# A gated-feed-forward kernel: casts and quantisation of its down stage shared out anew, and products that nobody reads put ahead of it

## What is computed

```python
x = x + jnp.tanh(g_xattn[0]) * _L0_xattn_ref(_layernorm(x, axis=-1), ctx_1024, ctx_1024, L0_xattn_w, L0_xattn_u)
x = x + jnp.tanh(g_ffn[0]) * _L0_ffn_ref(_layernorm(x, axis=-1), L0_ffn_clip_x, L0_ffn_clip_down, ...)

def _act_fake_quant(x, clip_factor):
    scale = jax.nn.sigmoid(clip_factor) * jnp.max(jnp.abs(x)) / QMAX
    return jnp.clip(_ste_round(x / scale), -QMAX - 1.0, QMAX) * scale
...
xq = _act_fake_quant(x, clip_x[0])
gate = jnp.einsum('bsh,ih->bsi', xq, _weight_fake_quant(w_gate))
up = jnp.einsum('bsh,ih->bsi', xq, _weight_fake_quant(w_up))
h = _act_fake_quant(jax.nn.silu(gate) * up, clip_down[0])
return jnp.einsum('bsi,hi->bsh', h, _weight_fake_quant(w_down))
```

## Time and profile before

| | |
|---|---|
| median of 3 runs | 224.18 us (224.08 to 225.59) |
| profiled execution | 224.41 us |
| its span, first to last instruction | 222.9 us |
| mean granted TensorE clock | 0.911 |
| busy: PE, DVE, ACT, POOL | 160.8, 171.0, 156.0, 138.5 us |

### The profile page before, as it was taken

How to read it: one execution, slowest core, us unless ns; L and a number is a source line. 1 busy time by engine, 2 the same in 40 slices (tenths; PEclk the granted TensorE clock), 3 DMA queues, 4 the chain that set the end, 5 groups by cost and what they waited for, 6 DMA issues and landing times.

```text
span 222.9 us, 3218 instructions
## 1 busy us (share of the span) xinstructions
PE 160.8 (72%) x1034; PEld 113.4 (51%) x1034; DVE 171.0 (77%) x344; ACT 156.0 (70%) x234; POOL 138.5 (62%) x157
## 2 busy tenths in 40 slices
PE   0002997799999999974066567949999952989960
PEld 0001342799999999964055452404343411766630
DVE  0689357445856779998679669677999998999992
ACT  3496596446698796996479966855988962899400
POOL 3467300425979999893688807992686670019991
PEclk9999999999999999999655766988999997699995
DMA  3999989999999878300000000000000000003458
GB/s 105 321 370 349 307 263 294 305 285 301 285 285 268 227 204 222 96 1 1 0 0 0 0 3 1 0 0 3 0 0 0 0 1 3 0 0 128 157 195 276
DMA packets 43327, 29.29 MB, mean 131 GB/s; under 512 B 2224, under 2 KB 43056, under 8 KB 43312
## 3 DMA queue, kind: packets, MB, share of 16 engines
q1 hardware_dynamic: 43168, 28.84, 44.8%
q10 hardware_dynamic: 144, 0.26, 0.3%
HBM read 24.65 MB, written 4.46 MB: 131 GB/s over the span
## 4 chain that ended last, share of the span: by engine, by line
PE 35%; DVE 17%; ACT 17%; POOL 11%; issue 9%; SPq 4%; DMA 4%; DVEq 1%; POOLq 0%; ACTq 0%
PE ps L955 11%; PE ps L988 8%; PE ps L884 6%; PE ps L868 5%; DMA hidden<-in_ctx 4%; SPq L261 4%; PE ps L908 3%; POOL x_all L389 3%; DVE h_space L831 2%; POOL hidden L382 2%; ACT hidden L563 2%; ACT silu_out L608 2%; DVE hidden L792 2%; DVE silu_out L700 2%; ACT h_space L608 2%
## 5 line engine op out<-in xcount | busy, mean ns | idle before, releaser
L884 PE MATMUL ps<-hidden 128*128 128x128 f32 (+1 forms) x512 | 58.5, 275 | 4.0 <-DVE hidden L638 2.5
L884 PEld LDWEIGHTS ps<-hidden 128*128 128x128 f32 x512 | 57.7, 192 | 5.2 <-issue 3.3
L868 PE MATMUL ps<-hidden,flip 128*128 128x512 f32 x32 | 16.7, 683 | 21.2 <-DMA hidden<-in_ctx 21.0
L389 POOL TENSOR_TENSOR x_all<-x_all,silu_out 128x512 f32<-128x512 f32 x16 | 24.4, 1536 | 10.8 <-DVE silu_out L700 10.7
L803 DVE TENSOR_REDUCE h_peaks<-hidden (+2 forms) x24 | 26.0, 1123 | 4.0 <-POOL hidden L433 3.2
L988 PE MATMUL ps<-wdT,z_t 128*128 128x256 bf16 (+1 forms) x192 | 25.3, 288 | 2.6 <-ACT z_t L622 2.6
L691 DVE SCALAR_TENSOR_TENSOR h_space<-z_t,ps 128x256 f32<-128x256 f32 x32 | 19.2, 599 | 10.3 <-PE ps L884 10.2
L908 PE MATMUL ps<-ident,hidden 128*128 128x128 f32 x64 | 14.3, 401 | 14.8 <-POOL hidden L413 11.1
L622 ACT ACTIVATE z_t<-h_space 128x1024 bf16<-128x1024 int8 (+3 forms) x12 | 20.1, 1756 | 6.6 <-DVE h_space L831 6.6
L988 PEld LDWEIGHTS ps<-wdT,z_t 128*128 128x128 bf16 (+1 forms) x192 | 17.2, 102 | 10.7 <-issue 4.8
L608 ACT ACTIVATE silu_out<-ps,mix_scale 128x1024 f32<-128x1024 f32 (+1 forms) x18 | 18.4, 1020 | 5.6 <-PE ps L955 2.6
(11 more groups left out here) (99 smaller groups left out, 331.6 us busy)
## 6 DMA issues: line engine op xcount, KB each, us to landing
hidden<-lag_w SPq DMA_DIRECT2D x26, 512.0 KB, 5.7
x_all<-in_x SPq DMA_DIRECT2D x8, 512.0 KB, 9.0
hidden<-in_ctx SPq DMA_DIRECT2D x8, 512.0 KB, 8.8
out<-x_all SPq DMA_DIRECT2D x16, 256.0 KB, 2.1
xq<-in_L_ffn_w_down SPq DMA_DIRECT2D x1, 704.0 KB, 5.7
xq<-in_L_ffn_w_gate SPq DMA_DIRECT2D x1, 640.0 KB, 6.5
h_space<-in_L_ffn_w_up SPq DMA_DIRECT2D x1, 640.0 KB, 5.7
lag_w<-up_out ACTq DMA_DIRECT2D x1, 255.0 KB, 7.8
```

Source lines behind the costliest of these rows:

```text
L389: nc.gpsimd.tensor_tensor(xs, xs, mixed[:, m % 2, :, :].rearrange("p c b -> p b c"), ALU.add).then_inc(s["x1_done"], 1)
L868: last = nc.tensor.matmul(turned(g)[:, half], flip[:, :], ring[g % SLOTS][:, half], start=True, stop=True)
L884: last = nc.tensor.matmul(ps[:, j % BANKS, c * 2 * SEQS:end * 2 * SEQS], lag_tile(j)[:, c, :], ekp[:, (j * CK + c) * 2 * SEQS:(j * CK + en ...
```

## The change

Five things change in the down stage, and block 0 keeps its six pieces.

1. Vector quantises only tiles 0 to 3 of blocks 1 to 3, in two pieces of 2048 columns.
2. ScalarE quantises tile 4 and the half tile (1536 columns, the new line 638) and then casts these, then tiles 0 and 1, then tile 2.
3. Pool casts tile 3 of blocks 1 to 3 (the new line 444): block 1's ahead of all additions, block 2's ahead of addition 4, block 3's ahead of addition 8.
4. TensorE multiplies a block in three parts, tiles 4 and 5, tiles 0 and 1, tiles 2 and 3; the last waits for ScalarE and for Pool. A semaphore, `row_read`, keeps block 1 from bank 6 until `down_row` has been read.
5. TensorE runs 14 products of 512 columns in bank 5 before the transpose of the peak and 8 after `row_ps`, which nobody reads (`idle_products`).

```diff
--- before.py
+++ after.py
@@ -159,13 +159,17 @@
         def z_bank(g):
             return (2, 6, 0)[g % 3]
 
-        def pieces(b):
-            return [(k, k + 1) for k in range(KA)] if b == 0 else [(0, KA // 2), (KA // 2, KA)]
-
-        def piece(b, k):
-
-            before = 0 if b == 0 else KA + 2 * (b - 1)
-            return before + (k + 1 if b == 0 else 1 + k // (KA // 2))
+
+
+        ACT_Q = 4
+
+        def quantised(b):
+
+            return KA + 2 * b
+
+        def act_cast(b):
+
+            return KA + 3 * b
 
         EVEN = (KA + 1) // 2
         ODD = KA // 2
@@ -222,9 +226,9 @@
             "top_done", "topT",
 
             "scale_x", "x8_done", "xq_done", "xq_cast", "gate_done", "up_done", "silu_done", "up_kept", "h_even", "h_odd",
-            "hpeak_done", "h_top_done", "h_topT", "row_ps",
-
-            "h8_done", "hq_done", "down_done", "ffn_done", "sum_done", "dve_sum_done", "out_done")}
+            "hpeak_done", "h_top_done", "h_topT", "row_ps", "row_read",
+
+            "h8_done", "h8_act", "hq_done", "hq_pool", "down_done", "ffn_done", "sum_done", "dve_sum_done", "out_done")}
 
         x_in = [sem(f"x_in{g}") for g in range(GROUPS)]
         ring_in = [sem(f"ring_in{i}") for i in range(SLOTS)]
@@ -434,7 +438,15 @@
                                             up_even[i % 2], ALU.mult).then_inc(s["h_even"], 1)
 
 
+            def cast_h(b):
+                pool.wait_ge(s["h8_done"], quantised(b))
+                wait(pool, s["down_done"], 4 * (b - 1))
+                nc.gpsimd.tensor_copy(hq[:, b % 2, 3 * BT:4 * BT], h8[:, b % 2, 3 * BT:4 * BT]).then_inc(s["hq_pool"], 1)
+
+            cast_h(1)
             for n in pool_sums:
+                if n in (4, 8):
+                    cast_h(n // 4 + 1)
                 pool.wait_ge(s["ffn_done"], n + 1)
                 xs = x_all[:, n * 2 * C:(n + 1) * 2 * C]
                 nc.gpsimd.tensor_tensor(xs, xs, ffn[n // 4 % 2][:, n % 4, :], ALU.add).then_inc(s["sum_done"], 1)
@@ -613,13 +625,25 @@
                                              scale=mix_scale[:, 1, k:k + 1]).then_inc(s["up_kept"], 1)
 
 
-            for b in range(BLOCKS):
-                for k, end in pieces(b):
-                    act.wait_ge(s["h8_done"], piece(b, k))
-                    if k == 0:
-                        wait(act, s["down_done"], 4 * (b - 1))
-                    cols = slice(k * BT, min(end * BT, HB))
-                    nc.scalar.activation(hq[:, b % 2, cols], h8[:, b % 2, cols], ACT.Copy).then_inc(s["hq_done"], 1)
+            def cast_h(b, k, end):
+                cols = slice(k * BT, min(end * BT, HB))
+                nc.scalar.activation(hq[:, b % 2, cols], h8[:, b % 2, cols], ACT.Copy).then_inc(s["hq_done"], 1)
+
+            for k in range(KA):
+                act.wait_ge(s["h8_done"], k + 1)
+                cast_h(0, k, k + 1)
+            for b in range(1, BLOCKS):
+                first, last = ACT_Q * BT, HB
+                wait(act, s["hq_done"], KA if b == 2 else act_cast(b - 2) if b > 2 else 0)
+                nc.scalar.activation(h8[:, b % 2, first:last], hidden[:, b * HB + first:b * HB + last], ACT.Copy,
+                                     scale=S["inv_h"]).then_inc(s["h8_act"], 1)
+                act.wait_ge(s["h8_act"], b)
+                wait(act, s["down_done"], 4 * (b - 1))
+                cast_h(b, ACT_Q, KA)
+                act.wait_ge(s["h8_done"], quantised(b) - 1)
+                cast_h(b, 0, 2)
+                act.wait_ge(s["h8_done"], quantised(b))
+                cast_h(b, 2, 3)
 
 
         @block.vector
@@ -824,9 +848,10 @@
 
             def quantise_h(b):
 
-                for k, end in pieces(b):
-                    if k == 0:
-                        wait(dve, s["hq_done"], piece(b - 2, KA - 1) if b >= 2 else 0)
+                if b >= 2:
+                    dve.wait_ge(s["hq_done"], act_cast(b - 2))
+                    wait(dve, s["hq_pool"], b - 2)
+                for k, end in [(k, k + 1) for k in range(KA)] if b == 0 else [(0, 2), (2, 4)]:
                     last = min(end * BT, HB)
                     nc.vector.tensor_scalar(h8[:, b % 2, k * BT:last], hidden[:, b * HB + k * BT:b * HB + last],
                                             S["inv_h"], None, ALU.mult).then_inc(s["h8_done"], 1)
@@ -837,6 +862,7 @@
             dve.wait_ge(s["row_ps"], 1)
             for j in range(2):
                 link(nc.vector.tensor_scalar(down_row[:, j, :], ps[:, 6, 0:C], S["out_scale"], None, ALU.mult))
+            nc.vector.sem_inc(s["row_read"], 1)
             quantise_h(1)
 
             for b in range(BLOCKS):
@@ -931,6 +957,11 @@
             pe.sem_inc(s["silu_done"], 2)
             pe.wait_ge(s["z_kept"], GROUPS - 1)
 
+            def idle_products(n):
+
+                for i in range(n):
+                    nc.tensor.matmul(ps[:, 5, :], ident_b[:, :], wgT[:, 0, 0:512], start=True, stop=True)
+
             def gate_up(b):
 
                 for k in range(KA):
@@ -959,22 +990,31 @@
             for b in range(BLOCKS):
                 gate_up(b)
 
+            idle_products(14)
             pe.wait_ge(s["h_odd"], ODD * (BLOCKS + 1))
             every_partition("h_top")
 
             for h in range(CH):
                 last = nc.tensor.matmul(ps[:, 6, h * P:(h + 1) * P], ones[:, :], down_diag[:, h, :], start=True, stop=True)
             last.then_inc(s["row_ps"], 1)
+            idle_products(8)
 
 
 
             def down(b, sl):
 
-                for first, end in pieces(b):
-                    pe.wait_ge(s["hq_done"], piece(b, first))
+                for n, (first, end) in enumerate([(k, k + 1) for k in range(KA)] if b == 0 else [(4, KA), (0, 2), (2, 4)]):
+                    if b == 0:
+                        pe.wait_ge(s["hq_done"], n + 1)
+                    else:
+                        pe.wait_ge(s["hq_done"], act_cast(b - 1) + n + 1)
+                        if end == 4:
+                            pe.wait_ge(s["hq_pool"], b)
                     for i in range(4):
-                        if first == 0:
+                        if n == 0:
                             wait(pe, s["ffn_done"], 4 * (b - 2) + i + 1)
+                            if b == 1 and i == 2:
+                                pe.wait_ge(s["row_read"], 1)
                         for k in range(first, end):
                             for j in range(2):
                                 t = 2 * i + j
@@ -986,9 +1026,10 @@
                                     col = KI * BT + t * P % (BT // 2)
                                     lhs, rhs = hq[rows_, sl, col:col + P], wdT[rows_, KI, :]
                                 last = nc.tensor.matmul(ps[:, 4 * sl + i, j * C:(j + 1) * C], lhs, rhs,
-                                                        start=(k == 0 and j == 0), stop=(k == KA - 1),
+                                                        start=(n == 0 and k == first and j == 0),
+                                                        stop=(end == (KA if b == 0 else 4) and k == end - 1),
                                                         skip_group_check=True)
-                        if end == KA:
+                        if end == (KA if b == 0 else 4):
                             last.then_inc(s["down_done"], 1)
 
             for b in range(BLOCKS):
```

## The result

The changed kernel takes 225.11 us in the median of 12 runs, where the one before takes 224.46 on the same chip in 12. The forecast was 224.5 us, +0.35. The medians differ by 0.65 us (a ratio of 1.0029) and the means, 225.16 and 224.37, by 0.79. The measured ratios in this document compare fast runs alone and so aren't quotients of the medians; here it is 1.0064, with an interval of 1.0035 to 1.0093. By each of these the changed kernel is a little slower, within one per cent, and by about twice the forecast or more.

A forecast was written before the change was run, and what follows sets the result against it. Pool's queue of additions, releasing store 9 ahead of a full store pipe, was taken to bound the down stage. Its terms put the tenth addition at 215.9 against 215.51, so 224.18 + 0.35 = 224.5 us, range 223.7 to 225.5.

The forecast's parts named there:

- the tenth addition: Pool's down-stage residual addition that releases store 9; predicted to end at 215.9 against 215.51, with a full store pipe behind.
- ScalarE's quantisation: After block 0's casts, ScalarE's quantisation of 1536 columns was to take 1.56 us, bounds 1.47 and 2.5.
- casts 2 and 3: Pool's casts ahead of additions 4 and 8, 1.0 us each from start to start, bounds 1.0 and 1.49.
- block 3's quantisations: Vector's two pieces for block 3 were to block Pool 2 x 0.97 us instead of 1.50 + 1.25.
- Vector's lead: Ahead of the additions: block 0's evictions at 197.9 instead of 198.74, Pool at 198.7 instead of 199.50; bounds 0.4 to 1.6.
- The sum as printed: Pool's queue to its tenth addition: 198.7 + 12.35 + 2.0 + 1.94 + 0.9 = 215.9, given as +0.35 us.
- The clock falls in block 1: Rival: TensorE idles 194.2 to 196.6, then runs at low clock; half the block 225.0 us, whole 227.5; chances 0.07, 0.03.
- Products may be late by about 2 us: Slack in the down stage before additions 12 and 13 miss their places behind store 9.
- The rule for the price: Low clock in block 1: half the block loses 2.5 us; the whole loses 5, of which 3 are seen.
- the products alone set the end: Rival: down products end the program, so block 1's start 0.4 us earlier is the whole effect, 223.8 us; chance 0.16.
- ScalarE never bounded: Rival that ScalarE bounds the blocks: 2.5 us quantisation, 6.6 us a block, 224.5 to 225.5 us; chance 0.04.
- Dearer casts: Rival: Pool's casts cost 1.49 us each beyond the blocking, giving 225.5 to 226.0 us; chance 0.12.

The follow-up runs named there:

- cast 2 early: Changed kernel with Pool's cast of block 2 right behind that of block 1, ahead of the first addition: median 225.23 us, ratio 1.0057.
- stores 10 and 11 first: Changed kernel with the stores of n = 10 and 11 issued ahead of 8 and 9: median 224.97 us, stretch 38.02.
- no Pool casts: Changed kernel with tile 3 cast by ScalarE together with tile 2, and no cast on Pool: median 224.45 us, stretch 36.58.
- half tile second: Kernel before, with the half tile multiplied ahead of tiles 3 and 4 in blocks 1 to 3: median 224.83 us, stretch 36.96.
- changed again: Changed kernel, unedited, run once more with another profiled execution: median 225.49 us, stretch 38.05.
- both best guesses: Changed kernel without idle products, block 2's cast early, sum 7 on Vector, stores 10, 8, 11, 9; the second also multiplies blocks in four parts: 223.96 and 223.68 us.
- the gap bridged: Changed kernel with 7 more idle products between blocks 0 and 1: median 224.86 us, stretch 37.08, and 37.05 in another execution.

## Why the prediction was wrong

**What held.** The end is the tenth addition plus a full pipe of stores, for as long as the products aren't much later. In ten of the 17 profiles, the two of the comparison among them, the stretch ends 7.35 to 7.38 us behind store 9; in the other seven (cast 2 early, stores 10 and 11 first, no Pool casts, half tile second, changed again, both best guesses) it ends 4.29 to 4.31 us behind store 13, and later than a full pipe behind the tenth store would have it. Store 9 waits for Pool's queue. Store 13 waits for Pool's last addition, and in six of the seven Pool is idle ahead of its last two until block 3's evictions come; in the half tile second it is addition 12 that takes longer. The terms of the sum, predicted and measured: ScalarE's quantisation 1.56 and 1.56; casts 2 and 3 at 1.0 and 1.0; block 3's quantisations hold Pool up by 0.97 each and by 0.99 and 0.98; block 1's first product at 196.6 and 196.59 (195.53 + 1.06). Vector's lead was to be 0.84 and is 0.70; 0.12 of the missing 0.14 lies between `down_row` and the next quantisation, where the signal of `row_read` stands (191.41 + 1.06 against 192.35). The sum as printed comes to 215.89, +0.38, and the shorter lead makes up the rest of the way to +0.46, within 0.06.

By the Trainium skill, SBUF — State Buffer, section "Who interferes with whom", the second to ask for the shared ports waits for the whole instruction. The changed trace agrees: 2.06 us for Vector's 1.28, 2.02 for Pool's 1.03.

**The step that failed** is the clock in block 1, which the sum has at nothing and the rival "The clock falls in block 1" at chances of 0.07 and 0.03. The clock was low in block 1 in both profiles of the changed kernel and in all three edits of it that left the gap and the order as they were, for 3.4 us three times and 6.8 us twice. I had the mechanism, its place and the slack. "Products may be late by about 2 us" is borne out: 1.25 and 1.67 us late cost nothing, 2.72 late cost 1.0 us. What I read wrongly was the evidence. The idle stretch at 38 us that kept the clock, and the work at 145.5 to 148.9 that didn't, showed that it can go either way, and the change turned a gap of 0.68 us into one of 1.90. How long TensorE is idle doesn't decide it: a gap of 2.33 us kept the clock once and lost it once, and the idle stretch at 38 us, which kept it, was 2.46 long. The timeline of TensorE in the kernel before, behind that stretch:

```profile
40.35 5.82 PE L884 MATMUL ps<-hidden 128*128 128x128 f32 x50 [2.46 <-DVE hidden L638]
```

The rule for the price held and its size was off: half a block slow was to lose 2.5 us, of which all but about 2 is seen, +0.5 over the forecast. In the long case block 1 takes 9.28 us instead of 6.25, so 3.0 are lost, and 38.05 is 1.0 over 37.06.

**What it adds up to.** Where the low stretch is absent or short, Pool's queue costs the 0.46 us. In the long case store 9 is as early as before (29.23), and the products alone put the end 1.45 us over that of before. Two of the five profiles of the changed kernel and its like were the long case: some 0.9 us by these few. The medians are 0.65 and 1.2 us apart in the two comparisons, and the means over all runs 1.16, with a standard error near 0.2. Whole times don't show the clock's share by themselves. In means of 12, with standard errors of 0.3 to 0.4 each, the changed kernel is 0.79 and 0.98 us over the kernel before that ran beside it, and with the gap bridged it is still 0.87 over and without idle products 0.84, where the stretch says 0.5; with cast 2 early it is 1.34 over, and 0.53 with the gap bridged as well. So a third cost of a few tenths is not ruled out, and how often the long case comes in unprofiled runs stays open.

**Rivals.** That the products alone set the end, which would have given 223.8, fell with the half tile second: they ended 3.0 us earlier, and the program didn't. ScalarE never bounded: its four instructions take 5.7 us a block, under the 6.24 of the products. Dearer casts fell: 1.03 us each, where nothing blocked them.

## What to carry to other kernels

Take a chain of waits that names one engine for the whole stage as a question: look for what is issued last (here stores, in the order of a list), and follow back from the first point after which that pipe is full. When two engines share a port, a queue's length is its own work plus each instruction of the other that it meets, and making a third engine faster can move those meetings to a worse place. Idle products that keep TensorE's clock up ahead of a stage also let it run dry sooner inside the stage; look for the gap that this opens, and fill that one, or leave both out.

## What was not expected of the hardware

Products of 64 rows are cheaper together. A block whose eight products of 64 rows alternate in pairs with products of 128 rows takes 6.07 us (block 2 before, counted in the same way); with the eight in a row it takes 5.03 (block 2 of the half tile second, from its first product to block 3's), for the same 48 products.

The same program's clock differs between executions by when it changes level: the part between the two peaks' transposes took 53.3 us where it was low for 3.4 to 6.2 us of them, 54.7 where it was low for 7.1 to 7.3, and 55.7 to 56.0 where it was low for 10.2 to 11.6. A change of half a microsecond in a later stage can't be read from the whole time without a few dozen runs, and was read from single profiles by the right stretch.
